# Four-layer attention network on one core: one sequential chain against two chains woven into every engine's queue

## The chip, the core and the metric

The kernel runs on one NeuronCore of a Trainium2 chip. Its engines run their own instruction streams and meet only through semaphores: TensorE (PE, with its weight loads shown apart as PEld), VectorE (DVE), ScalarE (ACT), GpSimd (POOL) and SyncE (SP), which here issues all DMAs. The metric is the device time of one execution in microseconds (us).

## What is computed

Input `x` is 4 batches of 256 channels x 1024 tokens in fp32. Each batch goes through four layers, and no batch reads another:

```python
# L0: attention over 1024 tokens, 32-wide queries and keys; softmax over the keys
x = gamma * V(x) @ softmax(Q(x).T @ K(x)).T + x
# L1 and L3: group norm (32 groups), then full attention with 256-wide heads
h = group_norm(x); x = x + Wo @ (V(h) @ softmax(Q(h).T @ K(h) / 16).T)
# L2: layer norm over channels, causal attention with 8 heads of 32 and one shared key/value,
#     then wo, layer norm, layer norm, w1, layer norm, gelu, w2, and two residuals
```

The four layers of a batch depend on each other in order, L0, L1, L2, L3. The layers of different batches are independent.

## The kernel before

`build` (line 215) writes one program per engine. Each engine loops over the 4 batches (`Fori`) and in each runs L0, L1, the causal layer L2 and L3 one after the other. Channels lie in 2 tiles of 128 partitions, tokens in 8 tiles (`NT`) of 128.

**Precision.** Nearly every large product is made of fp32 values split into two fp32r parts, `hi` (rounded by ACT) and `lo` (the rest, subtracted on DVE), and three TensorE passes hi*hi, hi*lo, lo*hi (`PASSES`, line 568; `product`, line 585, whose only matmul line is 589). In the full attentions (`full_attention`, line 652 for PE) this holds for queries, scores, values (`vt`) and the transposed probabilities (`probsT`). The causal values (line 875) are plain fp32: a plain fp32 product that is not a transpose stands in the trace as two MATMUL records.

**A full layer.** `attention_order` (line 55) lists its steps: `v` values of the keys, `s` scores of one 128-query tile (1024 keys), `t` the eight transposes of its probabilities, `o` a quarter of the output product for a half of the queries. Per tile DVE takes the row maximum (1149 or 1152), ACT the exponential (926), DVE scales the row by its inverse sum (1160, 1161), PE transposes (670), ACT copies the result out as `probsT_hi` (918) and DVE subtracts `probsT_lo` (1120). L1 and L3 begin with a group norm: a chain of small DVE steps, one PE product (730), a power on POOL (544), then `h_hi` (974) and `h_lo` (1260).

**The causal layer.** `causal_schedule` (line 80) is one list walked by all engines: `max` (scores for the row maxima, PE 831 with the mask product 835, DVE 1375), `shift` (the maxima transposed and written under the queries by DMA, 842, 511), `exp` (scores again, 855, exponential 1030), `values` (875, diagonal tiles masked by POOL 560), `norm` (the division, 1403 to 1411), and the feed-forward part `wo` to `w2` in parts of 4, 2 and 2 token tiles (`PARTS`). It works on 512 queries and two heads at a time.

**Order and PSUM.** PSUM is a ring of 4 slots of two banks; `ring_units` (line 157) gives each product its slot, and `open_unit` (line 570) makes PE wait until the slot's last reader is done. Every engine takes its work in the order of these lists.

Of the kernel before, what the change touches and what calls it, by code (L numbers as in the profile page):

```python
# [5 lines left out]
F32 = mybir.dt.float32  # L6

F32R = mybir.dt.float32r  # L10
# [11 lines left out]
TPH = HALF // P  # L22
HEADS, DH = 8, 32
HG = 2
EPS_GN, EPS_LN = 1e-6, 1e-5
SLOTS = 4
ACC = 3

# [8 lines left out]
DVE_STEPS = 117  # L37


def causal_blocks():  # L40

    return [(0, 0), (1, 0), (0, 1), (1, 1)]
# [3 lines left out]

PARTS = [(0, 4), (4, 2), (6, 2)]
FEED_FORWARD = ("wo", "ln2b", "f1b", "ta", "w1", "f2b", "tg", "w2")
FILLS = ("xt", "xn", "q2", "kv", "vt", "wo", "ta", "w1", "tg", "w2")
LAG = 2  # L50

NORM_PIECES = 6


def attention_order(layer):

    if layer == "L0":
        out = [("v", 0), ("s", 0), ("s", 1), ("s", 2), ("v", 1)]
    else:
        out = [("v", 0), ("v", 1), ("s", 0), ("s", 1), ("q", 1), ("v", 2), ("s", 2), ("v", 3)]
    for i in range(NT):
        out.append(("t", i))
        if i + 3 < NT:
            out.append(("s", i + 3))
        if TPH - 1 <= i < NT - 1:
            out.append(("o", 0, i - TPH + 1))  # L70
    if layer != "L1":

        out[-2:] = [out[-1], out[-2]]
    last = [("o", 1, i) for i in range(TPH)]
    if layer == "L1":
        last = [("xt", 0), last[0], last[1], ("xn", 0), last[2], ("q2", 0), last[3]]
    return out + last


def causal_schedule():  # L80

    blocks = causal_blocks()

    def max_events(k):
        hg, ib = blocks[k]
        out = []
        for t in range(TPH * ib, TPH * (ib + 1)):
            end = (t + 1) * P
            for ch, (lo, hi) in enumerate([(0, end)] if end <= HALF else [(0, HALF), (HALF, end)]):  # L100
                out += [("max", k, t, ch, lo, hi, pair) for pair in range(2)]
        return out


    first = sorted(max_events(0), key=lambda e: e[-1])
    step = 0
    ahead = [max_events(k) for k in range(len(blocks))]
    events = [("kv", 0), ("xt", 1), ("vt", 0)] + first[:4] + [("xn", 1)] + first[4:6] + [("q2", 1)]
    events += first[6:7] + [("kv", 1)] + first[7:] + ahead[1][:2] + [("shift", 0), ("vt", 1)] + ahead[1][2:]


    fill = [
        evenly(ahead[2][:3] + [("shift", 1)] + ahead[2][3:8], 11),
        evenly(ahead[2][8:] + ahead[3][:2] + [("shift", 2)] + ahead[3][2:5], 11),
        evenly(ahead[3][5:] + [("shift", 3), ("wo", 0)], 18),
        list(zip((1, 4, 9, 12, 13, 18, 21), [(e, 0) for e in FEED_FORWARD[1:]])),
    ]
    pending = []
    divide = []
    for k, (hg, ib) in enumerate(blocks):  # L120
        base = []
        for jt in range(TPH * (ib + 1)):
            base += [("exp", k, jt, pair, step) for pair in range(2)]
# [3 lines left out]
            step += 1  # L127
        for i, e in enumerate(base):
            events.append(e)
            events += [f for at, f in fill[k] if at == i]  # L130
            if divide:
                events.append(divide.pop(0))
            if e[0] == "values" and e[1] < k and e[2] == TPH * (blocks[k - 1][1] + 1) - 1:
                divide = norm(k - 1)
        assert not divide
    return events + pending + norm(len(blocks) - 1) + [(e, part) for e in FEED_FORWARD for part in (1, 2)]


def evenly(events, places):

    return [(i * places // len(events), e) for i, e in enumerate(events)]
# [6 lines left out]
def event_name(e):  # L148

    if len(e) == 2:  # L150
        return f"L2.{e[0]}{e[1]}"
    if e[0] == "values":
        return f"L2.o{e[1]}"
    return "L2." + ".".join(map(str, e[:4] + e[-1:]))


def ring_units():


    units = []  # L160
    last = [-1] * SLOTS

    def add(name, eng, held):

        s = min((s for s in range(SLOTS) if s != ACC or not held), key=lambda s: last[s])
        last[s] = len(units)
        units.append((name, eng, s, (0, 1)))

    def accumulated(name, eng, banks):
        last[ACC] = len(units)  # L170
        units.append((name, eng, ACC, banks))

    def attention(l):
        held = False
        for e in attention_order(l):

            held = held or e == ("s", NT - 2)
            if e[0] == "o":
                ct, j0 = divmod(e[2] * TPH, NT)
                if j0 + TPH == NT:  # L180
                    accumulated(f"{l}.o{e[1]}{ct}", "dve", (ct,))
            elif e[0] in ("xt", "xn", "q2"):
                add(event_name(e), "act" if e[0] == "xt" else "dve", held)
            else:
                add(f"{l}.{e[0]}{e[1]}", "act" if e[0] == "s" else "dve", held)

    add("L0.q", "dve", False)
    add("L0.k", "dve", False)
    attention("L0")
    for l in ("L1", "L3"):  # L190
        if l == "L3":
            held = False
            for e in causal_schedule():
                if e[0] == "norm" or len(e) == 2 and e[0] not in FILLS + ("shift",):
                    continue
                if e[0] == "values":
                    held = True
                    if e[2] == TPH * (causal_blocks()[e[1]][1] + 1) - 1:
                        accumulated(event_name(e), "act", (0, 1))
                        held = e[1] + 1 < len(causal_blocks())  # L200
                else:
                    add(event_name(e), "act" if e[0] in ("xt", "shift", "exp", "tg", "w2") else "dve", held)
        add(f"{l}.gn", "dve", False)
        add(f"{l}.q0", "dve", False)
        attention(l)
    return units


def split_units(units):

    kinds = ("q", "k", "v", "t", "xn", "kv", "ta")
    return [u[0] for u in units if u[0].split(".")[1].rstrip("0123456789") in kinds]


def build(nc, t):

    units = ring_units()
    number = {u[0]: i for i, u in enumerate(units)}
    reader = {u[0]: u[1] for u in units}
    where = {u[0]: u[2:] for u in units}  # L220
    U = len(units)

    rank, total = {}, {"act": 0, "dve": 0}
    for name, eng, _, _ in units:
        total[eng] += 1
        rank[name] = total[eng]
    halves = split_units(units)
    half_no = {name: i for i, name in enumerate(halves)}
    SPLITS = len(halves)
    schedule = causal_schedule()  # L230
    blocks = causal_blocks()

    norms = ["L1.gn", "L2.ln1.0", "L2.ln1.1"]
    for e in schedule:
        if e[0] in ("wo", "ln2b", "w1"):
            norms.append("L2.%s.%d" % ({"wo": "ln2", "ln2b": "f1", "w1": "f2"}[e[0]], e[1]))
    norms.append("L3.gn")
    H_PARTS = 5
    ready = [("xn", 0), ("xn", 1)] + [e for e in schedule if e[0] in ("ta", "tg")]
    norm_no = {name: i for i, name in enumerate(norms)}  # L240
    NORMS = len(norms)
    diagonal = [e for e in schedule if e[0] == "exp" and e[2] >= TPH * blocks[e[1]][1]]
    DIAG = len(diagonal)
    last_max = {e[1]: e for e in schedule if e[0] == "max"}

    first_max = {next(e for e in schedule if e[0] == "max" and blocks[e[1]][1] == ib and e[-1] == two): (ib, two)
                 for ib in range(NB) for two in range(2)}
    diag_no = {event_name(e): i for i, e in enumerate(diagonal)}

    with ExitStack() as ctx:  # L250
        def sem(name):
            return ctx.enter_context(nc.semaphore(name))

# [9 lines left out]
        def place(name, shape, at, dtype=F32):  # L263
            size = 2 if dtype == BF16 else 4
            for d in shape[1:]:
                size *= d
            return nc.alloc_sbuf_tensor_at(name, shape, dtype, offset=at), at + size

        def shared(name, shape, at, dtype=F32):
            return place(name, shape, at, dtype)[0]  # L270

        def sb(name, shape, dtype=F32):
            tensor, end = place(name, shape, top[0], dtype)
            top[0] = (end + 31) // 32 * 32
            return tensor
# [9 lines left out]

        KIB = 1024
        r_xin, r_x, r_q, r_k, r_v = region(8), region(8), region(16), region(16), region(16)
        r_p, r_t, r_s = region(8), region(64), region(8)

        xin = shared("xin", [P, CT, N], r_xin)  # L290
        x = shared("x", [P, CT, N], r_x)

# [1187 lines left out]
```

## Time and profile before

| | |
|---|---|
| time, median of 3 runs | 1571.64 us (1568.68 to 1576.68) |
| profiled execution: time, span | 1572.43 us, 1570.7 us |
| PE busy | 1326.2 us, 84% of the span |
| DVE busy | 1008.6 us, 64% |
| ACT busy | 567.8 us, 36% |
| POOL busy | 122.8 us, 8% |
| mean granted TensorE clock | 0.898 |

The page gives busy time per engine, the costliest groups of instructions by line, and the waits. Matmuls overlap in the pipeline: the record of one 128x512 product lasts some 390 ns, while the next starts 227 ns later. What PE needs for a piece of work is therefore read from the distance between starts, not from the length of a record. The granted clock of a stretch says which part of 2.4 GHz TensorE was given; 0.5 is the lower of its two levels, 1.2 GHz.

### The profile page before, as it was taken

Reading aid. Unit: us, or ns where it says so; the run is one execution under the profiler, and the core shown is the slowest. Engines: PE = TensorE matmul, PEld = TensorE weight load, DVE = VectorE, ACT = ScalarE, POOL = GpSimd, SP = SyncE. Lnnn points to the kernel's source line nnn. Section 1 sums busy time; section 2 is a strip of 40 time slices with the busy share of each in tenths; the row PEclk is TensorE's granted clock in tenths of the full one; section 3 lists DMA queues with packets and bytes.
Section 4 is the critical chain, followed back from the end, with each engine's and each line's share of the span. In section 5 each row is a group of like instructions: output and inputs, shape, how many; then the busy total and the mean of one; then the engine's idle time right before and its main releaser. Section 6 shows DMA issues by size and latency. Waiting matters only on the chain.

```text
span 1570.7 us, 21594 instructions
## 1 busy us (share of the span) xinstructions
PE 1326.2 (84%) x7440; PEld 999.4 (64%) x7440; DVE 1008.6 (64%) x1913; ACT 567.8 (36%) x777; POOL 122.8 (8%) x314
## 2 busy tenths in 40 slices
PE   5789888958978988984998898896798898889688
PEld 4568664547866865444876776544686687645577
DVE  2647568666565756866656565877575565696665
ACT  2324224514342423452434331452343242245143
POOL 0000011210000001121000000212000000112100
PEclk9789979989979987997998997998798899799699
DMA  4000110000000011000000003000000001100000
GB/s 140 1 27 1 41 42 2 2 1 1 29 1 27 1 44 39 2 1 1 1 29 1 27 0 82 2 1 1 1 1 29 1 1 38 45 1 2 1 1 27
DMA packets 16393, 27.20 MB, mean 17 GB/s; under 512 B 2576, under 2 KB 6800, under 8 KB 16272
## 3 DMA queue, kind: packets, MB, share of 16 engines
q1 hardware_dynamic: 16272, 25.66, 5.9%
q8 instruction: 67, 1.10, 0.3%
q14 instruction: 54, 0.44, 0.1%
HBM read 8.61 MB, written 4.19 MB: 8 GB/s over the span
## 4 chain that ended last, share of the span: by engine, by line
issue 88%; POOL 7%; PE 4%; POOLq 0%; DVE 0%; ACT 0%
PE ring L589 3%; POOL cprobs L560 3%; POOL rstd L544 2%; POOL idle_pool L559 2%; PE ring L670 0%; POOLq L426 0%; PE ring L738 0%; POOLq L543 0%; PE ring L743 0%; ACT h_hi L974 0%; DVE x L1174 0%; POOLq L547 0%; DVE gn_nb L1250 0%; DVE gn_msc L1249 0%; DVE gn_sc L1248 0%
## 5 line engine op out<-in xcount | busy, mean ns | idle before, releaser
L1030 ACT ACTIVATE cprobs<-ring 128x1024 f32<-128x1024 f32 (+1 forms) x192 | 152.1, 812 | 206.3 <-PE ring L855 205.8
L589 PE MATMUL ring<-probsT_hi,vt_hi 128*128 128x512 f32 x384 | 158.2, 412 | 11.9 <-DVE probsT_lo L1120 11.6
L918 ACT ACTIVATE probsT_hi<-ring 128x1024 fp32r<-128x1024 f32 x96 | 98.1, 1026 | 188.4 <-PE ring L670 188.0
L1120 DVE TENSOR_TENSOR probsT_lo<-ring,probsT_hi 128x1024 fp32r<-128x1024 f32 x96 | 116.5, 1221 | 67.0 <-ACT probsT_hi L918 67.0
L831 PE MATMUL ring<-ks,qs 96*128 96x512 f32 (+3 forms) x384 | 144.0, 452 | 17.9 <-DVE part_max L1375 6.1
L589 PE MATMUL ring<-probsT_hi,vt_lo 128*128 128x512 f32 x384 | 153.9, 401 | 0.0
L589 PE MATMUL ring<-probsT_lo,vt_hi 128*128 128x512 f32 x384 | 153.6, 400 | 0.0
L1375 DVE TENSOR_REDUCE part_max<-ring 128x2 f32<-128x1024 f32 (+3 forms) x128 | 127.3, 1017 | 35.1 <-PE ring L835 17.2
L855 PE MATMUL ring<-qs,ks 98*128 98x512 f32 (+3 forms) x384 | 115.6, 396 | 13.6 <-DVE part_max L1375 12.1
L544 POOL TENSOR_TENSOR rstd<-var_eps,half_neg 128x2 f32<-128x2 f32 (+1 forms) x52 | 46.2, 889 | 997.8 <-DVE var_eps L1245 548.1
L926 ACT ACTIVATE probs<-ring,neg_max 128x1024 f32<-128x1024 f32 x96 | 106.8, 1113 | 42.0 <-DVE neg_max L1154 38.8
L670 PE MATMUL ring<-consts,probs 128*128 128x128 f32 x768 | 107.6, 288 | 15.1 <-DVE probs L1161 15.0
L831 PEld LDWEIGHTS ring<-ks,qs 96*128 96x128 f32 x384 | 85.5, 232 | 53.3 <-DVE part_max L1375 16.9
L670 PEld LDWEIGHTS ring<-consts,probs 128*128 128x128 f32 x768 | 95.0, 149 | 31.5 <-DVE probs L1161 22.4
L855 PEld LDWEIGHTS ring<-qs,ks 98*128 98x128 f32 x384 | 65.3, 203 | 63.4 <-DVE part_max L1375 22.9
L589 PE MATMUL ring<-h_hi,q_hi 128*128 128x512 f32 x256 | 104.0, 406 | 0.4
L1152 DVE TENSOR_REDUCE shift_max<-ring 128x1 f32<-128x1024 f32 x64 | 78.4, 1225 | 38.8 <-PE ring L589 35.4
L589 PE MATMUL ring<-h_hi,q_lo 128*128 128x512 f32 x256 | 100.1, 391 | 0.0
L589 PE MATMUL ring<-h_lo,q_hi 128*128 128x512 f32 x256 | 100.0, 391 | 0.0
L589 PEld LDWEIGHTS ring<-probsT_hi,vt_hi 128*128 128x128 f32 x384 | 74.2, 193 | 35.1 <-DVE probsT_lo L1120 17.0
L875 PE MATMUL ring<-cprobs,v 128*32 128x512 f32 (+3 forms) x768 | 83.3, 506 | 3.1 <-ACT sums L1039 3.0
L589 PEld LDWEIGHTS ring<-probsT_hi,vt_lo 128*128 128x128 f32 x384 | 74.4, 194 | 16.2
(218 smaller groups left out, 2592.3 us busy)
## 6 DMA issues: line engine op xcount, KB each, us to landing
qs<-q_hi SPq DMA_DIRECT2D x64, 128.0 KB, 2.3
xin<-x_dram SPq DMA_DIRECT2D x4, 1024.0 KB, 5.1
qs<-q_lo SPq DMA_DIRECT2D x32, 128.0 KB, 2.3
out_dram<-x SPq DMA_DIRECT2D x8, 512.0 KB, 2.9
qs<-max_rows SPq DMA_DIRECT2D x64, 4.0 KB
raw_L_wv<-L_wv_dram SPq DMA_DIRECT2D x2, 256.0 KB, 6.2
raw_L_woT<-L_woT_dram SPq DMA_DIRECT2D x2, 256.0 KB, 6.3
raw_L_wq<-L_wq_dram SPq DMA_DIRECT2D x2, 256.0 KB, 6.6
```

Source lines behind the costliest of these rows:

```text
L544: pool.tensor_tensor(rstd[:, n, 0:w], var_eps[:, n, 0:w], half_neg[:, 0:w], ALU.pow).then_inc(rstd_ready, 1)
L589: ins = mm(out, w, m, start=first and n == 0, stop=last and n == len(every) - 1)
L670: last = nc.tensor.transpose(o[:, j, :], probs[:, ti % 2, j * P:(j + 1) * P], ident)
L831: last = mm(o[:, i, 0:hi - lo], qs[0:3 * DH, ib, 4 * hg + 2 * two + i, at:at + P], ks[0:3 * DH, lo:hi], start=True, stop=not diag)
L855: last = mm(o[:, i, 0:n], ks[0:3 * DH + 2, jt * P:(jt + 1) * P], qs[0:3 * DH + 2, ib, 4 * hg + 2 * two + i, HALF - n:HALF], start=True, st ...
L875: last = mm(acc[DH * a:DH * (a + 1), bank, HALF - n:HALF], w, causal_probs(step, a // 2, n)[:, a % 2, :], start=jt == 0, stop=jt == last_jt)
L918: A(dst, flat(name) if src is None else src, ACT.Identity, bias=bias, scale=scale).then_inc(hi_ready, 1)
L926: A(probs[:, ti % 2, :], flat(f"{l}.s{ti}"), ACT.Exp, bias=neg_max[:, ti:ti + 1], accum_out=row_sum[:, ti:ti + 1]).then_inc(act_read, 1)
L1030: A(causal_probs(step, two, n), slot(event_name(e))[:, :, 0:n], ACT.Exp).then_inc(act_read, 1)
L1120: ins = v.tensor_tensor(dst, src, f32(hi), ALU.subtract)
L1152: then(b, v.tensor_reduce(shift_max[:, ti:ti + 1], flat(f"{l}.s{ti}"), AX_X, ALU.max, negate=True))
L1375: v.tensor_reduce(cols if ti < TPH else parts[:, ch, :], slot(name)[:, :, 0:n], AX_X, ALU.max, negate=True).then_inc(dve_read, 1)
```

## The change

The kernel is written anew around two chains.

- The **full chain** runs the twelve full layers in the fixed order `FULL`; the **causal chain** runs the causal layers of batches 0, 1, 2, 3. The `Fori` loops are gone: everything is unrolled.
- Each engine's program is a weave of the two. `ORDER` holds one string per engine; each letter says from which chain the next step comes (for PE also at which PSUM bank it is placed). `weave` follows it. The order is fixed; no engine picks work while it runs. The chains meet where the causal layer of batch b reads the output of L1 of batch b, and L3 of batch b reads the output of the causal layer.
- Values in the full layers: `vt` and `probsT` are plain fp32. The `lo` parts and their DVE subtractions are gone, and the three fp32r passes of 512 queries become one fp32 product of 256 queries: 64 products of 128x256 per layer, where there were 96 of 128x512.
- In nine of the twelve full layers the scaling of the probabilities moves from DVE to ACT (`SCALED_BY`).
- The causal layer works on 256 queries and four heads at a time (8 blocks, 40 exp steps a batch), its feed-forward part on four parts of 2 tiles. The queries are stacked by 96 DMAs a batch (24 before), the shifts by 32 (16 before).
- PSUM: a ring of seven single banks shared by both chains, and one bank for the causal accumulation.
- Semaphores are kept apart for the two chains. The input of batches 0 and 1 is loaded at the start, and the splitting of the weights (`prepare`) lies in the causal chain, so that L0 of batch 0 begins without it.

```diff
+FULL = [("L0", 0), ("L1", 0), ("L0", 1), ("L1", 1), ("L0", 2), ("L3", 0), ("L1", 2), ("L0", 3), ("L3", 1), ("L1", 3),
+        ("L3", 2), ("L3", 3)]
+SCALED_BY = ["dve" if n in (0, 1, 11) else "act" for n in range(len(FULL))]
+ORDER = {
+    "PE": (
+        "0F2egF0c3F5Fac35F02F40F26FFF4F02F46FFF0F246FFF06FFF02F402F4F0242F04F20F46FFF2F04F26FFF0eF246FFF06FFFce0F2F0e"
...
+def weave(order, full, causal):
+    for ch in order:
+        next(full if ch in "F0123456" else causal)
+    assert next(full, None) is None and next(causal, None) is None
...
+            def full_values(l, b, qi):
+                wait_read(pe, full_name(l, b, ("t", 2 * qi + 1)))
+                o = open_unit(full_name(l, b, ("o", qi)))[:, 0, :]
+                for ct in range(CT):
+                    for j in range(NT):
+                        last = mm(o[:, ct * QUARTER:(ct + 1) * QUARTER], vt[:, j, ct * P:(ct + 1) * P],
+                                  probsT[:, qi % (NQ - 1), j, :], start=j == 0, stop=j == NT - 1)
+                        if ct == CT - 1 and j == NT - 1:
+                            last.then_inc(filled["f"], 1)
+                        if j % TPH == TPH - 1:
+                            yield
...
+            def scaled(n, ti):
+                act.wait_ge(row_sum_inverted, scaled_no(n, ti))
+                A(probs[:, ti % 2, :], probs[:, ti % 2, :], ACT.Identity,
+                  scale=row_inv[:, ti:ti + 1]).then_inc(probs_scaled["act"], 1)
+            def turned(l, b, ti):
+                name = full_name(l, b, ("t", ti))
+                wait_filled(act, name)
+                nc.scalar.copy(probsT[:, ti // 2 % (NQ - 1), :, (ti % 2) * P:(ti % 2 + 1) * P],
+                               slot(name).rearrange("p b (s n) -> p (b s) n", n=P)).then_inc(read_done["f", "act"], 1)
...
-            with pe.Fori(0, B) as b:
-                pe.wait_ge(h_lo, b * H_PARTS + 1)
...
-                full_attention(b, "L0")
-                group_normed(b, "L1")
-                causal_layer(b)
-                group_normed(b, "L3")
+            weave(ORDER["PE"], full_chain(), causal_chain())
```

The PE string has 1221 steps. Read along it, the first step of each causal layer cuts it into six stretches:

| stretch | steps | full layers in it | causal |
|---|---|---|---|
| head | 87 | L0.0, L1.0 up to its second output quarter | weights |
| C0 | 256 | rest of L1.0, L0.1, most of L1.1 | batch 0 |
| C1 | 303 | rest of L1.1, L0.2, L3.0, most of L1.2 | batch 1 |
| C2 | 304 | rest of L1.2, L0.3, L3.1, most of L1.3 | batch 2 |
| C3 | 223 | rest of L1.3, L3.2 | batch 3 |
| tail | 48 | L3.3 | none |

## Rows read from the trace of the kernel before

**Rows 1.** The page's busy times (us, share of the span, instructions).

```profile
PE 1326.2 (84%) x7440; PEld 999.4 (64%) x7440; DVE 1008.6 (64%) x1913; ACT 567.8 (36%) x777; POOL 122.8 (8%) x314
```

**Rows 2.** Windows, third batch: stretch, us, busy PE PEld DVE ACT POOL, clock, DMA.

```profile
808.00:872.00 64.00, 52.44 (x252) 43.12 (x250) 37.17 (x51) 21.39 (x28) 0.00 (x0) 0.87 0.04 10
872.00:950.00 78.00, 72.53 (x372) 60.52 (x372) 48.48 (x86) 29.48 (x42) 1.71 (x2) 0.96 0.05 16
950.00:1122.00 172.00, 135.86 (x888) 87.33 (x888) 121.65 (x271) 60.56 (x82) 28.91 (x75) 0.85 0.08 18
1122.00:1190.00 68.00, 66.74 (x337) 55.80 (x338) 42.48 (x63) 27.70 (x38) 0.00 (x0) 0.97 0.03 11
```

**Rows 3.** Timeline of PE, output products of L0: first and last of 21 (start, length).

```profile
99.80 0.39 PE L589 MATMUL ring<-probsT_hi,vt_hi 128*128 128x512 f32 x1
...
104.33 0.39 PE L589 MATMUL ring<-probsT_hi,vt_lo 128*128 128x512 f32 x1
```

**Rows 4.** Timeline of PE, products of 258 columns: first and last of 24.

```profile
116.14 0.28 PE L589 MATMUL ring<-L_wvo_hi,h_hi 128*128 128x258 f32 x1
...
118.88 0.28 PE L589 MATMUL ring<-L_wvo_hi,h_lo 128*128 128x258 f32 x1
```

**Rows 5.** Timeline of PE in L1: eight transposes and the next score products.

```profile
140.39 1.03 PE L670 MATMUL ring<-consts,probs 128*128 128x128 f32 x8
141.18 0.48 PE L589 MATMUL ring<-h_hi,q_hi 128*128 128x512 f32 x1
141.50 0.40 PE L589 MATMUL ring<-h_lo,q_hi 128*128 128x512 f32 x1
```

**Rows 6.** Timeline, weight preparation: four plain fp32 products of 256 columns (8 records).

```profile
25.69 1.89 PE L598 MATMUL ring<-raw_L_woT,raw_L_wv 128*128 128x256 f32 x8
...
27.42 0.50 PE L602 MATMUL ring<-vecs,raw_L_woT 128*128 128x1 f32 x4
```

**Rows 7.** Timeline of PE in the causal layer: values, then max, exp.

```profile
262.48 1.06 PE L875 MATMUL ring<-cprobs,v 128*32 128x512 f32 x8
...
264.34 0.44 PE L831 MATMUL ring<-ks,qs 96*128 96x384 f32 x1
...
264.96 0.70 PE L855 MATMUL ring<-qs,ks 98*128 98x512 f32 x2
```

**Rows 8.** Timeline of PE, first batch: L1, first causal step, L3, next L0.

```profile
107.15 0.38 PE L730 MATMUL ring<-gn_in,consts 128*128 128x4 f32 x2 [2.43 <-DVE gn_in L1238]
...
165.35 1.09 PE L763 MATMUL ring<-consts,x 128*128 128x128 f32 x8
...
356.74 0.38 PE L730 MATMUL ring<-gn_in,consts 128*128 128x4 f32 x2 [2.68 <-DVE gn_in L1238]
360.75 0.79 PE L738 MATMUL ring<-h_hi,L_wqk_hi 128*128 128x512 f32 x1 [3.63 <-ACT h_hi L974]
...
426.04 0.49 PE L589 MATMUL ring<-h_hi,wqk_hi 128*128 128x512 f32 x1
```

**Rows 9.** Groups by line and form, DVE then ACT (busy us, mean ns).

```profile
L1120 DVE TENSOR_TENSOR probsT_lo<-ring,probsT_hi 128x1024 fp32r<-128x1024 f32 x96 | 116.5, 1221 | 67.0 <-ACT probsT_hi L918 67.0
L1161 DVE TENSOR_SCALAR probs<-probs,row_inv 128x1024 f32<-128x1024 f32 x96 | 72.3, 753 | 3.4
L1042 ACT CAST h_hi<-xin 128x2048 fp32r<-128x2048 f32 x1 | 1.9, 1894 | 0.0
```

**Rows 10.** Timeline, all engines: load of the input, first product of L0.

```profile
9.44 0.54 SPq L493 DMA_DIRECT2D xin<-x_dram  x1
...
41.22 0.79 PE L589 MATMUL ring<-h_hi,wqk_hi 128*128 128x512 f32 x1 [7.87 <-DVE h_lo L1418]
```

**Rows 11.** Windows: start of a causal layer (columns as in rows 2).

```profile
208.00:220.00 12.00, 11.70 (x40) 8.61 (x41) 8.54 (x15) 2.03 (x3) 0.55 (x2) 0.50 0.43 100
```

**Rows 12.** Timeline of DVE, last layer: group norm begins; last residual.

```profile
1497.04 0.26 DVE L1233 BATCH_NORM_AGGREGATE gn_mv<-gn_stats 128x2 f32<-128x24 f32 x1
...
1566.79 0.75 DVE L1174 SCALAR_TENSOR_TENSOR x<-ring,L_bvo,x 128x512 f32<-128x512 f32 x1 [4.69 <-PE ring L589]
```

More of the change, by code:

```diff
@@ L22 @@
 TPH = HALF // P
+QUARTER = 256
+NQ = N // QUARTER
 HEADS, DH = 8, 32
@@ L63, in attention_order @@
     else:
[L64 to L76, printed above, removed]
@@ L77, in attention_order @@
-    return out + last
-def causal_schedule():
[L93 to L117, printed above, removed]
+        out = [("gn", 0), ("q", 0), ("v", 0), ("v", 1), ("s", 0), ("s", 1), ("q", 1), ("v", 2), ("v", 3), ("s", 2)]
@@ new lines, in evenly, with norm, fills @@
+def evenly(events, first, places):
+    return [(first + i * (places - first) // len(events), e) for i, e in enumerate(events)]
+def norm(k):
+    return [("norm", k, i) for i in range(NORM_PIECES)]
+def fills(k, places):
+    ahead = max_events(k + 2) + [("shift", k + 2)] if k + 2 < K else []
+    if k == 0:
+        ahead = [("xn", 1)] + ahead
+    elif k == 1:
+        ahead = [("q2", 1)] + ahead[:2] + [("kv", 1)] + ahead[2:] + [("vt", 1)]
+    out = evenly(ahead, 0, places) if ahead else []
+    part = k // 2 - 1
+    if part >= 0:
+        if k % 2 == 0:
+            late = ([("tg", part - 1), ("w2", part - 1)] if part else [])
+            out += evenly(late, 1, places - 1) if late else []
+            out.append((places - 1, ("wo", part)))
+        else:
+            out += evenly([(e, part) for e in FEED_FORWARD[1:6]], 0, places)
+    return out
@@ L127, in causal_schedule @@
             step += 1
+        fill = fills(k, len(base))
         for i, e in enumerate(base):
             events.append(e)
-            events += [f for at, f in fill[k] if at == i]
+            events += [f for at, f in fill if at == i]
             if divide:
                 events.append(divide.pop(0))
[L133 to L136, printed above, removed]
@@ L150, in event_name, with causal_name @@
+def causal_name(b, e):
     if len(e) == 2:
-        return f"L2.{e[0]}{e[1]}"
+        return f"C{b}.{e[0]}{e[1]}"
     if e[0] == "values":
[L153 to L206, printed above, removed]
@@ L209, in split_units @@
-def split_units(units):
-    kinds = ("q", "k", "v", "t", "xn", "kv", "ta")
-    return [u[0] for u in units if u[0].split(".")[1].rstrip("0123456789") in kinds]
-def build(nc, t):
[L217 to L229, printed above, removed]
-    schedule = causal_schedule()
-    blocks = causal_blocks()
-    norms = ["L1.gn", "L2.ln1.0", "L2.ln1.1"]
+        return f"C{b}.o{e[1]}"
@@ new lines, in queries, with ring_places @@
+def queries(k, jt):
+    return QUARTER - max(jt * P - BLOCKS[k][1] * QUARTER, 0)
+def ring_places(order):
+    full, causal = ([u for u in units if u[2]] for units in (full_units(), causal_units()))
+    queues = {"0123456": iter(full), "abcdefg": iter(causal)}
+    place, previous = {}, {}
+    holder = [None] * RING
+    for ch in order:
+        for banks, units in queues.items():
+            if ch in banks:
+                at = banks.index(ch)
+                name, _, width = next(units)
+                place[name] = at
+                before = [holder[i] for i in range(at, at + width) if holder[i]]
+                previous[name] = sorted(set(before), key=before.index)
+                holder[at:at + width] = [name] * width
+    return place, previous
@@ L590, in product, with both, project @@
                 return ins
-            def output_products(l, out):
+            def both(w):
+                return [lambda i, c, ms=slice(m * P, (m + 1) * P): w[i][:, c, ms] for m in range(CT)]
+            def project(name, weights, src, sl):
+                o = open_unit(name)
+                for bank, w in enumerate(weights):
+                    last = product(o[:, bank, :], [([w(i, c) for i in (0, 1)], [s[:, c, sl] for s in src])
+                                                   for c in range(CT)])
+                last.then_inc(filled[chain[name]], 1)
```

1748 lines of the change are left out of this document (974 added, 774 removed).

## Prediction

> **What bounds the kernel now.** I read the page's busy times first: PE is busy 84% of the span, DVE 64%, ACT 36% [rows 1]. The windows over one batch say where the other 16% lie [rows 2]: a batch takes 382 us, and PE is busy 52.4 of 64 us in L0, 72.5 of 78 in L1, 135.9 of 172 in the causal layer, 66.7 of 68 in L3. The granted clock tells the rest: 0.87, 0.96, 0.85 and 0.97. Busy time counts fill and slow clock as work, so I count what PE would need at full clock, from distances between starts. A 128x512 fp32r product takes (104.33 - 99.80)/20 = 0.2265 us [rows 3], one of 258 columns (118.88 - 116.14)/23 = 0.119 [rows 4], eight transposes 0.79 [rows 5].
>
> L1 or L3: 24 query, 96 score and 96 output products of 512 columns are 216 x 0.2265 = 48.9 us, 48 products of 256 columns 5.7, eight turns 6.3: 61. L0 has 16 score products in place of 96: 43. The causal layer: 36 products of 512 columns 8.2; 144 of 256 in wo, w1 and w2 17.1; 88 transposes 8.7; the identity products of w2 3.5; max and exp 36,864 columns each at 0.119 per 258, 17 + 17; 64 mask products at about 0.1 (two of 384 columns with their masks take 264.96 - 264.34 = 0.62, of which the columns are 0.35) 6.4; values 9,216 columns at 264.34 - 262.48 = 1.86 per 512 [rows 7] 33.5: 111. A batch holds 43 + 61 + 111 + 61 = 276 us of PE work and takes 382. So PE is the engine with most work, but 106 us of each batch, 28%, are waits, slow clock and switching, 61 of them in the causal layer, where DVE (121.7 of 172) and PE take turns. Four independent batches would be there to fill this.
>
> **The change part by part.** *Values in fp32.* A plain fp32 product of 256 columns is two records: eight records take 27.42 - 25.69 = 1.73 us, so one product 0.432 [rows 6]. A layer has 64 of these, 27.7 us, for 96 x 0.2265 = 21.7: +5.9 us a layer, **+71 us** of PE work over twelve layers. This is a loss where PE sets the pace, and PE will. What it buys is DVE time: 116.5 us of probsT_lo [rows 9], and a step less between the turn and the product.
>
> *PE work after.* L0 49, L1 and L3 67, causal 111 (the same columns; 256-query steps mask the same tiles), weight preparation 16. In all 4 x (49 + 67 + 111 + 67) + 16 = 1190 us. By the stretches of the PE string: head 114, C0 226, C1 292, C2 293, C3 197, tail 67.
>
> *Switching.* Work that starts after another kind costs a little: after the turn the first score product takes 0.32 instead of 0.23 [rows 3, 5]. As a check, L3 runs from 360.75 to 426.04 = 65.3 us [rows 8] with nearly no idle; less 1.7 for its first eight products at half clock, that is 2.6 above 61, or 0.08 for each of its some 31 units. The new string has 1221 steps; at 0.07 each +85 us. Bounds: 0 (a weight load that is pulled ahead, as between output products) and 0.09 (+110).
>
> *Other engines.* DVE loses 116.5 us of probsT_lo, about 25 of the value lo parts, and 72 of 96 scalings at 0.753, 54 [rows 9]: 1009 - 196 = 813 us, about 62% of the new time. ACT gains 72 scalings. No row shows ACT scaling SBUF to SBUF at this size; half of the 2048-column cast, 0.95 [rows 9], and the exponential with bias (1.11 for 1024) bound it, so 75 us at 1.05. Gelu now lies between exponentials of the other chain, so its table is loaded some 15 times more; no row here stands for that, and I count each like a scaling, +15. ACT: 568 + 90 = 658, half of the time. POOL is at 8% [rows 1] and keeps its selects and powers. SP issues 128 small DMAs a batch in the causal chain; at 0.54 an issue [rows 10] 69 us of 300. They are queued one and two blocks ahead, except at the start of a batch, where the first max waits for 12 issues, 6.5 us (6 before), and the full chain covers it. I cost all these at nothing in the mixed stretches; uncovered, the stacking would cost 3.2 us a batch more.
>
> *Waits added.* Every queue stays in order. A causal step whose data is late now also holds the full step behind it, on every engine, and the reverse; and seven PSUM banks serve both. What speaks against much of it is slack: scores run three tiles ahead of the turn, and one tile's chain (maximum 1.2, exponential 1.3, inversion 0.2, scaling 1.1, turn 0.8, copy 1.0 = 5.6 us) stands beside some 14 us of PE work per tile in a mixed stretch (67/8 full and about as much causal). I take 2% idle in C0 to C2, bounds 0 and 12% (below).
>
> *Head.* L0 began at 41.2 us because the weights of all layers came first [rows 10]. Its input is now the ninth load, issued near 4.5 us; with some 5 us of landing and the two halves' splitting PE starts near **14 us**. L0.0 has 49 us of work and 16 of preparation, and no partner: L0 took 64 to 66 us before at clock 0.87, with DVE the longer chain per tile; now PE is. I take 72. L1.0 up to the first causal step took (group norm at 107.2, first causal transposes at 165.4 [rows 8]) 58 us, and has about the same PE work, 49 against 50: 57. So C0 begins at 14 + 72 + 57 = **143**.
>
> *Mixed stretches.* C0 226 + 18, C1 292 + 21, C2 293 + 21 = 871; at 2% idle 889. C3 holds 197 + 16 = 213, while a causal layer alone lasts 191 (165.4 to 356.7 [rows 8], only its first 19 us beside L1's last products): two nearly equal limits, so 6% idle, 226.
>
> *Tail.* L3.3 alone: before, from its group norm at 1497.0 to the end at 1570.7, 73.7 [rows 12]; +5.9 for values, -5 because only the last quarter of the output (6.9) follows the last turn, not a half (10.9), and its residual is shorter: 75.
>
> **Sum.** 143 + 889 + 226 + 75 = 1333 us of span; the profiled execution stood 1.7 above its span and 0.8 above the median. Forecast **1335 us**, against 1571.6: 15% less. Cross-check: 1571.6 + 71 - 27 at the start = 1616, so 281 of today's 424 us (4 x 106) of waits, slow clock and switching have to go.
>
> **The rivals.**
> *Better overlap* (the lower bound): switching half as dear (-40) and 1% idle (-20): about **1273**. For it: output products with no switching cost; against it: rows 8.
> *Convoys in the fixed orders.* The string was laid out with some durations, and each difference on the chip makes an engine wait at the wrong step. If PE in C0 to C3 is held up 12% of the time instead of 2 to 6, 1084/0.88 = 1232, and the sum is 143 + 1232 + 75 + 2 = **1452**. L0 alone shows 82% busy now, L1 93%.
> *The clock stays down.* Short waits can leave TensorE at 1.2 GHz although it is almost always busy: 11.7 of 12 us busy at a clock of 0.50 at the start of a causal layer, against 66.7 of 68 at 0.97 in L3 [rows 2, 11]. If the mixed stretches had L0's and the causal layer's mean of about 0.87 [rows 2], 1084/0.87 = 1246: about **1466**. The Trainium skill ("TensorE: Matmul & The Clock Gate", section "A second HAM failure mode: psum-queue depth-cycling") says that a stream of matmul groups cycling through PSUM banks idles briefly between groups and so makes the clock swing between its levels. By that rule this case comes true; the row of L3, which cycles through the ring too at 0.97, speaks against it.
> *Slower than before.* One mechanism: a late causal step at the head of the PE queue holds up the full chain so often that the chains don't overlap. The causal layer today has PE busy 79% [rows 2]. If the mixed stretches only reach that, 1084/0.79 = 1372, the total is **1592**. The point from which it decides is 1572 - 143 - 75 - 2 = 1352 us in the mixed stretches, PE doing its dense work 80% of the time. Against it: the waits of the causal layer are for its own DVE and ACT steps, and full work stands between those steps now.
>
> **How the numbers follow.** Forecast (1290 to 1385): 0.58. Better overlap (1240 to 1290): 0.15. Convoys or between forecast and them (1385 to 1500): 0.16. Clock: 0.06. Slower: 0.04. No change: 0.01. The 8-in-10 range takes in better overlap to 1262 and convoys to 1440. A measurement of this kernel tells about 0.5% from no change; faster by more than that 0.95, within 0.01, slower 0.04.
>
> **What would show it.** First product of L0 near 14 us; first causal transposes near 143 (too late: the head). The output products: 12 x 128 records 0.216 apart. From 143 to 1260 PE busy over 97% at a clock of 0.97 or more (a clock of 0.87: that rival; PE idle before waits on DVE or ACT of the other chain: convoys). C0 near 249 us, C1 and C2 near 320, C3 near 226; DVE near 813 us busy, ACT near 658; a tail of 75 after the last w2 of batch 3. The prediction is wrong at its root if PE is busy all the time and the stretches are still longer: then the cost of switching is mis-sized.

## The result and the profile after

The change makes the kernel slower: 1633.3 us against 1570.2 for the kernel before (medians of four runs each), a ratio of 1.041 with a 95% interval of 1.038 to 1.044. I had forecast 1335, range 1262 to 1440, and given "slower" 0.04.

The profiled execution of the changed kernel has a span of 1632.3 us and a mean granted clock of 0.916. Its page: busy times (as rows 1), and the granted clock in 40 slices.

```profile
PE 1385.3 (85%) x9152; PEld 1102.3 (68%) x9152; DVE 817.3 (50%) x1782; ACT 666.0 (41%) x949; POOL 91.3 (6%) x134
PEclk9889959999998699999999779999999878999999
```

The work is what the forecast said: DVE 817 (forecast 813), ACT 666 (658). PE is busy for 85% of the span, no more than before [rows 1]; 1632.3 - 1385.3 = 247 us are idle. The windows by stretch, from one first causal step to the next (columns as in rows 2):

```profile
0.00:155.50 155.50, 126.88 (x644) 109.46 (x645) 65.29 (x136) 52.85 (x88) 1.06 (x7) 0.92 0.13 43
155.50:471.40 315.90, 268.13 (x1904) 208.79 (x1903) 172.58 (x377) 136.87 (x189) 22.05 (x31) 0.90 0.05 14
471.40:867.90 396.50, 338.09 (x2260) 269.00 (x2259) 196.73 (x428) 169.03 (x235) 22.76 (x32) 0.92 0.05 14
867.90:1263.80 395.90, 338.48 (x2266) 269.04 (x2265) 197.50 (x430) 170.94 (x238) 22.72 (x32) 0.92 0.04 12
1263.80:1549.00 285.20, 241.95 (x1724) 184.52 (x1722) 154.43 (x351) 109.97 (x158) 21.98 (x31) 0.90 0.06 16
1549.00:1632.00 83.00, 71.79 (x362) 61.53 (x362) 30.75 (x61) 26.36 (x41) 0.70 (x1) 0.95 0.04 13
```

The timeline of PE answers rows 10 (first product), rows 8 (group norm of L1.0, first causal step) and rows 6 (32 records of plain fp32 products, then the next score product):

```profile
13.21 0.77 PE L658 MATMUL ring<-h_hi,wqk_hi 128*128 128x512 f32 x1 [13.21 <-DVE h_lo L1341]
...
98.52 0.59 PE L727 MATMUL ring<-gn_in,consts 128*128 128x4 f32 x2 [2.64 <-DVE gn_in L1295]
...
133.08 7.07 PE L709 MATMUL ring<-probsT,vt 128*128 128x256 f32 x32
139.80 0.58 PE L658 MATMUL ring<-h_hi,q_hi 128*128 128x512 f32 x1
...
155.52 1.04 PE L850 MATMUL ring<-consts,x 128*128 128x128 f32 x8
```

| stretch | forecast us | measured us | PE idle in it |
|---|---|---|---|
| to the first product | 14 | 13.2 | |
| L0.0 and preparation | 72 | 98.5 - 13.2 = 85.3 | |
| L1.0 to the first causal step | 57 | 155.5 - 98.5 = 57.0 | |
| C0 | 249 | 315.9 | 47.8 |
| C1 | 320 | 396.5 | 58.4 |
| C2 | 320 | 395.9 | 57.4 |
| C3 | 226 | 285.2 | 43.3 |
| tail | 75 | 83.0 | 11.2 |

So the miss is in the mixed stretches: 1393.5 us where 1115 were forecast. PE is idle there for 206.9 us, 15%, where I had taken 2% (6% in C3), and the granted clock is 0.90 to 0.92 where I had taken no loss. Where does PE wait? The longest stall of each causal layer stands at its start. The issues of SP in C2, and the PE records between them with the ACT record that writes the maxima of block 0 (start, length, in brackets the idle time ahead). A *stack* is the set of 12 DMAs that brings the queries of one block together, a *shift* the 4 DMAs that write its maxima under them:

```profile
910.91 4.97 SPq L574 DMA_DIRECT2D qs<-q_hi  x8
915.93 2.49 SPq L574 DMA_DIRECT2D qs<-q_lo  x4
...
933.67 5.68 SPq L574 DMA_DIRECT2D qs<-q_hi  x8
939.38 2.49 SPq L574 DMA_DIRECT2D qs<-q_lo  x4
941.92 4.86 SPq L582 DMA_DIRECT2D qs<-max_rows  x8
```

```profile
914.27 0.71 PE L689 MATMUL ring<-ks,qs 96*128 96x512 f32 x2
919.76 0.44 PE L918 MATMUL ring<-ks,qs 96*128 96x128 f32 x1 [4.77 <-DMA qs<-q_lo]
...
927.35 0.44 PE L918 MATMUL ring<-ks,qs 96*128 96x128 f32 x1 [4.16 <-issue]
...
931.24 0.36 ACT L1150 CAST max_rows<-ring 8x256 fp32r<-8x256 f32 x1 [7.89 <-PE ring L879]
...
945.42 1.22 PE L931 MATMUL ring<-qs,ks 98*128 98x256 f32 x4 [10.52 <-DMA qs<-max_rows]
```

SP issues all four stacks, 48 DMAs in 31.0 us, from 910.9 to 941.9, and only then the shifts. ACT had the maxima of block 0 ready at 931.6. PE waits three times, for the first stack (4.8 us), for the second (4.2; the view names no releaser there, but the last issue of that stack ends at 926.0) and for the shift (10.5). The window of this stretch in the changed kernel:

```profile
910.90:945.40 34.50, 14.58 (x76) 11.86 (x76) 10.70 (x19) 8.15 (x13) 0.00 (x0) 0.59 0.18 47
```

PE is busy 14.6 of 34.5 us, at a clock of 0.59. The same stretch, from the first stacking DMA to the first exponents, stands in all four batches (34.7, 34.2, 34.5 and 35.1 us long). But the full chain had work. Why it did not fill the stretch is the question of the experiments.

### The profile page after: what moved, and what is told of

Its sections match the earlier page's. It is cut to its first block, busy times and chain, and to the rows that moved or that the text cites. A ratio compares the mean times of both kernels' runs of the same rounds, so it can differ in the third digit from the quotient of the medians.

```text
span 1632.3 us, 22497 instructions
## 1 busy us (share of the span) xinstructions
PE 1385.3 (85%) x9152; PEld 1102.3 (68%) x9152; DVE 817.3 (50%) x1782; ACT 666.0 (41%) x949; POOL 91.3 (6%) x134
## 4 chain that ended last, share of the span: by engine, by line
PE 71%; DVE 9%; SPq 8%; ACT 7%; issue 3%; DMA 1%; POOL 0%; DVEq 0%; ACTq 0%
PE ring L658 23%; PE ring L709 21%; PE ring L949 7%; SPq L574 7%; PE ring L931 5%; PE ring L701 4%; PE ring L918 4%; DVE part_max L1534 2%; PE ring L737 2%; ACT probsT L1018 1%; ACT cprobs L1175 1%; ACT probs L1007 1%; PE ring L858 1%; PE ring L893 1%; PE ring L920 1%
## 5 line engine op out<-in xcount | busy, mean ns | idle before, releaser
L709 PE MATMUL ring<-probsT,vt 128*128 128x256 f32 x1536 | 363.3, 393 | 36.6 <-ACT probsT L1018 34.4
L709 PEld LDWEIGHTS ring<-probsT,vt 128*128 128x128 f32 x1536 | 297.1, 197 | 85.4 <-ACT probsT L1018 39.1
L931 PE MATMUL ring<-qs,ks 98*128 98x256 f32 (+1 forms) x640 | 116.8, 307 | 49.0 <-DMA qs<-max_rows 40.3
L1534 DVE TENSOR_REDUCE part_max<-ring 128x2 f32<-128x1024 f32 (+2 forms) x112 | 127.2, 1137 | 43.7 <-PE ring L918 26.0
L931 PEld LDWEIGHTS ring<-qs,ks 98*128 98x128 f32 x640 | 92.1, 198 | 82.3 <-DMA qs<-max_rows 41.9
L1018 ACT COPY probsT<-ring 128x1024 f32<-128x1024 f32 x96 | 96.4, 1008 | 69.5 <-PE ring L701 69.5
L949 PE MATMUL ring<-cprobs,v 128*32 128x256 f32 (+1 forms) x1280 | 97.6, 377 | 2.9 <-ACT nums L1183 2.9
L949 PE MATMUL ring<-cprobs,ones 128*32 128x256 f32 (+1 forms) x1280 | 93.6, 365 | 0.0
L1012 ACT ACTIVATE probs<-probs,row_inv 128x1024 f32<-128x1024 f32 x72 | 82.9, 1151 | 21.7 <-DVE row_inv L1257 21.5
L1534 DVE TENSOR_REDUCE cmax<-ring 128x2 f32<-128x768 f32 (+3 forms) x48 | 49.9, 1044 | 60.6 <-PE ring L920 59.8
```

The costliest lines, as they stand in the source:

```text
L709: last = mm(o[:, ct * QUARTER:(ct + 1) * QUARTER], vt[:, j, ct * P:(ct + 1) * P], probsT[:, qi % (NQ - 1), j, :], start=j == 0, stop=j == ...
L931: last = mm(heads(name)[:, a, 0:n], ks[0:3 * DH + 2, jt * P:(jt + 1) * P], qs[0:3 * DH + 2, k % STACKS, a, QUARTER - n:QUARTER], start=Tru ...
L949: last = mm(acc[DH * a:DH * (a + 1), (half + 1) * QUARTER - n:(half + 1) * QUARTER], w, causal_probs(step, n)[:, a, :], start=jt == 0 and ...
L1012: A(probs[:, ti % 2, :], probs[:, ti % 2, :], ACT.Identity, scale=row_inv[:, ti:ti + 1]).then_inc(probs_scaled["act"], 1)
L1018: nc.scalar.copy(probsT[:, ti // 2 % (NQ - 1), :, (ti % 2) * P:(ti % 2 + 1) * P], slot(name).rearrange("p b (s n) -> p (b s) n", n=P)).the ...
L1534: v.tensor_reduce(cols if ti < TPH else parts[:, ch, :], src[:, :, 0:n], AX_X, ALU.max, negate=True).then_inc(read_done["c", "dve"], 1)
```

## Experiments

**Two attempts on the transfers.** First, only SP's order, so that the shifts don't queue behind the stacks of blocks 2 and 3:

```diff
-                    for k in range(STACKS):
-                        yield from stacks(b, k)
+                    yield from stacks(b, 0)
+                    yield from stacks(b, 1)
                     yield from shifts(b, 0)
                     yield from shifts(b, 1)
+                    yield from stacks(b, 2)
+                    yield from stacks(b, 3)
```

> Edit to the changed kernel: at the start of each causal layer SP issues the stacks of blocks 0 and 1, then the shifts of blocks 0 and 1, and only then the stacks of blocks 2 and 3 (before: all four stacks, then the shifts). Nothing else. Theory A, SP's queue holds up the first exponents: in C2 the row of maxima of block 0 stands ready at 931.6 us, its four transfers are issued from 941.9 and the first exponents start at 945.4. With the edit they should start some 9 us sooner in each of the 4 causal layers: 20 to 40 us less in all, part of it in granted clock, and the wait of TensorE for max_rows falls from 40.3 us to under 15. Against it works that the stacks of blocks 2 and 3 come 5 us later, so the wait for q_lo may grow. Rival B, each chain stands in an order written for other durations and the gap only moves on: under 8 us less.

Second, the same and half the transfers at this place:

```diff
+            def stack_pair(b, k):
...
+                        sp.dma_start(qs[DH * g:DH * (g + 1), k:k + 2, a, :].bitcast(F32),
+                                     src[DH * a:DH * (a + 1), :, token_quarter(qi)].bitcast(F32)
+                                     ).then_inc(stack_in[k], 16)
```

> As the shift-first kernel, and the stacks of blocks 0 and 1 (and those of 2 and 3) come in one set of 12 transfers of 64 KB in place of 24 of 32 KB: 24 issues less in each causal layer, 0.6 us each. Theory A: the maxima of block 1 no longer wait for the second stack, the first exponents start some 15 us sooner than in the changed kernel: 45 to 80 us less in all. Rival B: under 15 us less than the changed kernel, the time comes back as waits of TensorE for DVE and ACT.

Measured: 1624.9 us (ratio to the kernel before 1.033, 1.030 to 1.036), 8 us less than the changed kernel, and 1610.1 us (1.025, 1.022 to 1.028), 23 less. The first exponents of C2 start 25.6 and 21.8 us after the first stacking DMA, in place of 34.5, so the edit did what it should. The waits of PE, first in the changed kernel, then in the first attempt (engine, line waited at, releaser: us in total, times, longest):

```profile
PE ring L931 <- DMA qs<-max_rows: 40.3, 4, 11.1
PE ring L918 <- issue: 19.2, 5, 4.8
PE ring L918 <- DMA qs<-q_lo: 14.5, 3, 4.9
```

```profile
PE ring L920 <- issue: 34.1, 7, 7.5
PE ring L920 <- DMA qs<-q_lo: 33.4, 5, 10.6
```

The 40 us for `max_rows` are gone, and 34 have come back at the next stacks. In size theory A missed (20 to 40 and 45 to 80 were expected); rival B, the gap only moves on, gave under 8 for the first and under 15 for the second, and is near the first and short of the second: neither sum was right. The transfers are where PE waits, but making them come sooner recovers little while the strings stay as they are.

**Is there anything to weave?** The serial kernel keeps all steps and replaces the five strings, so that on every engine the chains stand one behind the other.

> The changed kernel's steps, banks and waits, but on every engine the two chains stand one behind the other (L0.0, preparation, L1.0, C0, L0.1, L1.1, L0.2, L3.0, C1, L1.2, L0.3, L3.1, C2, L1.3, L3.2, C3, L3.3): what the weaving itself brings. Theory A: the weave has cover to give (TensorE's work at full clock is 1190 us, its switches 85), so without it the time is well above the changed kernel's 1633: 1720 to 1800. Rival C, the weave costs about what it brings, because at each point where both chains could go on the fixed order makes one wait for the other: 1620 to 1680.

Measured: 2002.2 us (ratio 1.274, 1.269 to 1.279), above both ranges. Its page:

```profile
PE 1503.6 (75%) x9152; PEld 1176.1 (59%) x9152; DVE 824.8 (41%) x1782; ACT 662.9 (33%) x943; POOL 91.7 (5%) x134
```

PE is idle 2002.4 - 1503.6 = 499 us. The weave as changed saves 369 us, so rival C falls; theory A holds in its sign, while the time lies 200 us above its range. The kernel before reached 1570 without two chains. Part of the difference is the causal layer: alone it takes some 255 us here in batch 0 (from PE's first step in it at 182.2 to the first product of L0.1 at 437.4), where the old form took 191 [rows 8]. Which of its parts (256 queries, 128 small DMAs a batch, four heads) costs the 64 us was not tested.

**How much of PE's work is on the path?** Two lines:

```diff
-        vt = shared("vt", [P, NT, C], r_v)
+        vt = shared("vt", [P, NT, C], r_v, F32R)
-        probsT = shared("probsT", [P, NQ - 1, NT, QUARTER], r_t)
+        probsT = shared("probsT", [P, NQ - 1, NT, QUARTER], r_t, F32R)
```

> The changed kernel with the full layers' values and probabilities in fp32r in place of fp32 (one pass instead of four; the low parts are left out, so the output is less exact): 768 products of 128x256 at 0.12 in place of 0.43 us, 240 us less work on TensorE and nothing else changed. Theory D, TensorE's queue is the bound and its gaps are few: 1633 - 240 = 1393, within 30. Theory A (other engines and SP's queue set most gaps, and they stay where they are or grow when TensorE is quicker): only some 100 to 160 us less, 1475 to 1535, with TensorE's busy share down to some 77%.

Measured: 1442.3 us (ratio 0.918, 0.915 to 0.920), 191 us less for some 240 us less work, between the two expectations, so neither holds as stated. PE's idle time rose from 247 to 1440.2 - 1158.8 = 281 us. Most of PE's work does set the time, and the idle time lies on top of it.

**New strings by the same rule.** If the strings are wrong, new ones must be enough. I laid them out by walking the five queues with the durations of the changed kernel's trace: each instruction's time, the 0.62 us of a DMA issue, its landing, some 0.05 us from an end to the waiting engine's start, and PE at half clock after idle stretches, as the trace has it. At each point an engine takes the next causal step if its waits are over, else the full one, else it waits. The first 108 letters for PE:

```diff
 ORDER = {
     "PE": (
-        "0F2egF0c3F5Fac35F02F40F26FFF4F02F46FFF0F246FFF06FFF02F402F4F0242F04F20F46FFF2F04F26FFF0eF246FFF06FFFce0F2F0e"
+        "agcag2F0F20F4F20F42F04F26FFF2F40F26FFF2F046FFF46FFF64F024F2F0424F20F42F06FFF0F24F06FFF0eF426FFF26FFFce0F2Feg"
...
```

> Only the five strings of ORDER differ from the changed kernel (and with them the banks of the ring). The rule is the one of the changed kernel, the causal chain first wherever both can go on, but the order is laid out with the durations, issue times and landing times that the trace of the changed kernel shows: walking all five queues with them, each engine takes the causal step if its waits are over at that time, else the full one, else it waits for the first of the two. The same walk with the changed kernel's own strings ends at 1618 us (measured span 1632). Theory E, convoys: the old strings fit other durations, so the heads of the queues wait for each other although other steps could go on; with strings that fit, the walk ends at 1532, so 1535 to 1555. Rival F, the gaps are there because both chains are out of ready work or because the rule itself is bad: 1600 or more.

Measured: 1537.6 us (ratio 0.978, 0.973 to 0.984). Theory E holds (1535 to 1555), rival F falls. The same steps, 96 us less than the changed kernel and some 2% less than the kernel before. (That the changed kernel's own strings follow the same rule is a reading of them, not known.) Its windows for the start of C2, its page and its wait:

```profile
860.90:896.70 35.80, 31.34 (x188) 26.21 (x186) 16.40 (x30) 22.52 (x31) 0.00 (x0) 0.95 0.17 45
```

```profile
PE 1360.7 (89%) x9152; PEld 1082.1 (70%) x9152; DVE 812.9 (53%) x1782; ACT 666.0 (43%) x949; POOL 92.6 (6%) x134
```

```profile
PE ring L936 <- DMA qs<-max_rows: 1.3, 2, 0.8
```

The stacking takes as long as before, 35.8 us from its first issue to the first exponents. Now PE is busy 31.3 of them at a clock of 0.95. The reason can be read in the strings. From the first `max` of C2 to its first `exp` the changed kernel has `gegec24Fga`: three steps of the full chain (`2`, `4`, `F`). The new one has `ga40F26eaeFaFF0F42F06FFa`: seventeen. PE could not have done more in the changed kernel, since the head of its queue was a causal step and the next full step stood behind it. PE's share is not the whole difference, since the strings of the other engines were laid out anew with it.

**Another rule.** With the same durations, the step goes first from which the longer chain of work leads to the end:

> Again only the strings of ORDER differ. The rule is another one: where both chains can go on, the step goes first from which the longer chain of work leads to the end (with some offsets by stretch, chosen by trying), all with the durations of the trace of the changed kernel. The walk ends at 1419 us. Theory E: 1425 to 1450, TensorE's waits down from 252 to some 125 us, granted clock up to about 0.97; the values in fp32, the small stackings and the switching are all still there, so the loss against the kernel before was not theirs. Rival G, small differences of real durations from run to run bring the convoys back in any fixed string: 1500 to 1600.

Measured: 1433.0 us (ratio 0.914, 0.907 to 0.921). Theory E holds, rival G falls.

```profile
PE 1318.3 (92%) x9152; PEld 1054.4 (74%) x9152; DVE 812.4 (57%) x1782; ACT 663.5 (46%) x949; POOL 92.0 (6%) x134
PEclk9999999999999989999999999999999999999599
```

PE idle 112.8 us, mean clock 0.971. In all, 200 us lie between two orders of the same 1221 PE steps.

Two things set this order apart. In C2 only six full steps stand between the first `max` and the first `exp`, and still PE is busy for all of the 52.5 us from the first stacking DMA (838.9) to the first exponents (891.4), at a clock of 1.00: 29 more full steps stand ahead of the first `max`, behind the `q2` that lets SP begin the stacks. So the work to count is that from `q2` on. And the second largest wait of PE in the changed kernel, for ACT's copies of the turned probabilities, is nearly gone; the causal-first order still has 31.7 us of it. The changed kernel, then the longest-chain order:

```profile
PE ring L709 <- ACT probsT L1018: 34.4, 20, 3.6
```

```profile
PE ring L714 <- ACT probsT L1023: 6.7, 7, 2.0
```

**Which price was wrong?** The same layout by the causal-first rule, with one duration falsified on paper: 0.1 us for an issue of SP, then 0.3, and as a control 0.12 us for the output products. Only the strings differ on the chip.

> Only the strings of ORDER differ from the changed kernel. Rule and durations are those of the causal-first layout that ran in 1538 us, with one price changed on paper: while the strings are laid out, every DMA issue of SP counts 0.1 us in place of the 0.6 that it takes. On the chip nothing else changes. Theory H, this one price accounts for most of the changed kernel's loss: the strings believe that the stackings are there some 30 us sooner at each start of a causal layer and put causal steps at the heads of all queues before their data can be there. The layout itself believes in 1465 us; walked with the true issue time it ends at 1631, so 1630 to 1650 on the chip, what the changed kernel takes. Rival I, an order is forgiving towards one wrong price of an engine that is not the bound (SP's issues are 20% of the span): within 20 us of the 1538.

> As the kernel that priced SP's issues at 0.1 us, but with 0.3 on paper, half of what they take. Theory H: the loss goes with the lead that the layout believes in (stackings believed ready some 15 us early in place of 25): the walk with true durations ends at 1556, so 1555 to 1580, between 1538 (price right) and 1635 (0.1). Rival L, the loss comes from one accident of the strings and not from the price: no order between the three.

> Control for the kernel whose layout priced SP's issues at 0.1 us: the same rule (causal first) and the measured durations, but on paper the 768 output products of the full layers take 0.12 us in place of 0.43, so the layout leaves out 240 us of work of the busiest engine and believes in 1253 us. On the chip nothing but the strings differs. Theory H (a wrong price hurts where it says that something is ready which is not; too little work on the busiest engine only puts its neighbours a little off): the walk with true durations ends at 1559, so 1555 to 1580. Rival K, any large wrong price spoils the strings, and this one is the larger in sum (240 us against 256): 1620 or more.

The third column counts PE's full steps in C2 from the first `max` to the first `exp`, and from `q2` to the first `exp`. The fourth sums PE's idle time over the four starts, each from the first stacking DMA to the first exponents.

| kernel | SP issue / output product on paper | full steps from `max` / from `q2`, C2 | PE idle at the four starts | span estimated by the walk | measured median |
|---|---|---|---|---|---|
| changed kernel | unknown | 3 / 10 | 75 | 1618 | 1633.3 |
| issue cheap | 0.1 / 0.43 | 5 / 11 | 70 | 1631 | 1635.5 |
| issue at half | 0.3 / 0.43 | 10 / 16 | 54 | 1556 | 1576.1 |
| causal first | 0.62 / 0.43 | 17 / 28 | 15 | 1532 | 1537.6 |
| values cheap | 0.62 / 0.12 | 27 / 38 | 22 | 1559 | 1551.0 |

With the issue priced at 0.1 us the kernel takes what the changed kernel takes. Its windows at the start of C2 and its waits show the same stall:

```profile
911.50:945.60 34.10, 16.96 (x93) 14.18 (x91) 10.79 (x19) 9.08 (x14) 0.00 (x0) 0.62 0.18 47
```

```profile
PE ring L936 <- DMA qs<-max_rows: 38.0, 4, 10.1
PE ring L923 <- issue: 31.9, 8, 4.8
```

At 0.3 it is 1576.1 (ratio 1.004, 1.002 to 1.007), with this wait:

```profile
PE ring L936 <- DMA qs<-max_rows: 32.0, 4, 9.9
```

The control, wrong by 240 us of the busiest engine's work, costs 13 us against the right price (1551.0; ratio 0.989, 0.984 to 0.995). So the loss follows the price of the issue in order, and the one other price that was tried, as wrong in sum, hardly matters: theory H holds, rivals I, K and L fall. A wrong price for the landing, or for a step of DVE or ACT, was not tried. (The 1576.1 is at the upper edge of what was expected, the control a little below its range.) A price that is too low for PE's own full work puts too many full steps between causal ones, and they still do useful work (in the C2 start of this kernel PE is busy 44.8 of 51.8 us). A price that is too low for a transfer puts the waiting step at the head of the queue.

That the changed kernel's own strings were laid out with such a price is argued from the likeness (the full steps in the gap, the waits, the time). It was not shown, since how they were made isn't known.

**Both together.** The pair transfers with strings laid out for them by the longest-chain rule:

> The transfers of the pairs kernel (stacks of two blocks in one set of 12, shifts of blocks 0 and 1 ahead of the stacks of blocks 2 and 3) together with strings laid out for them by the longest-chain rule with measured durations. The walk ends at 1395 us. Theory E: 1400 to 1425. With the changed kernel's own strings these transfers brought 23 us against 1633, here 15 to 35 against the 1433 of the longest-chain layout. Rival J, in a fitting order the stackings are hidden anyway: 1428 or more.

Measured: 1416.6 us (ratio 0.901, 0.897 to 0.906), the fastest kernel of this study, 10% below the kernel before. Theory E holds, rival J falls.

```profile
PE 1311.0 (93%) x9152; PEld 1049.4 (74%) x9152; DVE 815.0 (58%) x1782; ACT 664.7 (47%) x949; POOL 91.5 (6%) x134
```

The transfers with strings of their own bring 16 us here, the transfers alone 23 with the old strings: a small matter in both, next to the order.

## Why the prediction was wrong

*What held.* The work: a plain fp32 product costs what rows 6 said (32 records in 139.80 - 133.08 = 6.72 to 7.07 us; forecast 6.9), and DVE and ACT came out within 8 us. The first product and L1.0 came within 1 us. L0.0 with the preparation was 13 us short: PE was busy 73.6 of its 85.3 us, where I had 65 of work. The tail was 8 short; I did not take it apart. One reading was wrong without harm: I wrote that no row stands for a load of ACT's table, but the kernel before has 17 of them at 1.28 us each, and the changed kernel 31.

*The step that failed* is "SP issues 128 small DMAs a batch ... They are queued one and two blocks ahead, except at the start of a batch, where the first max waits for 12 issues ... and the full chain covers it. I cost all these at nothing". Two things are wrong in it. The first exponents wait for 48 + 4 issues, since the shift stands behind all four stacks in SP's queue; I followed the queue only to the first max. And the full chain covers nothing that the string does not put there. I had 0.54 us an issue [rows 10] and the strings before me (the small issues took 0.62 to 0.65). 52 issues at 0.54 are 28 us; between the first `max` and the first `exp` the string of PE holds three full steps, eight transposes and two score products, with about 0.79 + 2 x 0.2265 = 1.2 us of work [rows 3, 5]. The two numbers were never laid side by side.

*What it cost.* The start of each causal layer lost 21, 20, 20 and 14 us of PE idle time (34.5 - 14.6 in C2), 75 of the 207. The causal-first layout, with that priced rightly, takes 96 us less. Between the two profiled executions, 59 us of that are idle time at the four starts (75 against 15), 12 are idle time elsewhere, and 25 are PE's busy time for the same instructions (1385.3 against 1360.7), at a clock of 0.945 for 0.916. So the start is the largest part of what a right price brings. It is not most of the idle time: the other 132 of the 207 us lie elsewhere in the mixed stretches, and what each wait there costs was not tested one by one. The granted clock was a consequence of the order, since only the strings differ: 0.59 in the stretch where PE is busy 42% of the time, 0.95 in the same stretch of the new strings at 88%. "No clock loss" failed with "2% idle". The clock rival had 0.87 for the mixed stretches; they came at 0.90 to 0.92. The rule of the Trainium skill that stood beside it ("TensorE: Matmul & The Clock Gate", section "A second HAM failure mode: psum-queue depth-cycling") is not borne out as the cause: the longest-chain kernel cycles through the same seven banks at a mean of 0.971.

*The rivals.* "Slower than before" named the right mechanism, a late causal step at the head of PE's queue that holds up the full chain, and the right threshold: it decides at PE doing its dense work 80% of the time, and 1084 / 1393.5 is 78%. I gave it 0.04. Its own price (1592) mixed two measures: 79% was the busy share of the old causal layer, slow clock included, while 1084 is work at full clock, and in that measure the old layer had 111 / 172 = 65%. I argued against it that full work stands between the causal steps, which is true of the chain and not of the string. "Convoys", at 12% idle, is the same mechanism at a smaller size; 15% idle and the clock came.

*Without the failing step.* The best strings that I found for the change's own steps give 1433, not 1335. PE is then idle 113 us of 1431, 8%, at a clock of 0.971. So 200 of the 298 us of error are the order. The other 98 are two terms: my sum had 1333 - 1190 - 85 = 58 us of idle time in all, and 113 were measured; and it had 1190 + 85 = 1275 us of work with its switches at full clock, and PE was busy 1318. The clock can account for most of these 43 us: a mean of 0.971 over 1431 us is some 83 us at the lower level, which costs at most 41, an estimate. So the price of switching is not refuted, nor is it shown by itself. No layout tried here comes near 2% of idle time. The +71 us for fp32 values and the +85 for switching don't explain the loss: both are still there at 1433.

## What to carry to other kernels

A woven program is only as good as the prices with which its order was laid out. Before judging one, take each long transfer or wait of one chain and count in the order string how much work of the other chain stands between the step that lets it begin and the first step that needs it. Follow a DMA queue to the last transfer that a consumer needs, not to the first; an issue is work of its queue even when it moves 2 KB. When a stall shrinks but the time doesn't, lay the order out anew before looking for the next stall.

## What the runs showed of the hardware

The small DMAs of the causal layer take SP some 0.62 us each, and their size hardly matters: in the rows above eight of 32 KB take 4.97 and 5.68 us and eight of 2 KB (`max_rows`) 4.86; in the kernel before two of 128 KB take 1.24. Eight of 64 KB in the pairs kernel follow, with the landing times of both sizes (KB each, median us from issue to landing). It is no constant of the queue: single transfers of 512 KB to 1 MB took 0.37 to 0.67 us to issue in the changed kernel.

```profile
893.39 5.17 SPq L587 DMA_DIRECT2D qs<-q_hi  x8
```

```profile
qs<-q_hi SPq DMA_DIRECT2D x64, 64.0 KB, 2.0
qs<-q_hi SPq DMA_DIRECT2D x128, 32.0 KB, 1.8
```

From issue to landing it is 1.8 us, or 2.0 for twice the bytes. The Trainium skill ("DMA: Bandwidth & Descriptors", section "Anatomy of one DMA — SWDGE (gpsimd) path") puts the sequencer's dispatch at about 50 ns, for GpSimd's path, on which no run here issues. On SP's queue the rows say 0.6 us, and an order laid out with 0.1 us costs 98 us. ACT's scaling between two SBUF tiles, which no row of before showed, takes 1.15 us for 1024 columns (estimate 1.05). And durations from one profiled execution were enough to lay out an order: the six layouts ran within 22 us of the walk's estimate, and the executions of each within 1.2% of one another.
